# A fused convolution, attention and mixture-of-experts kernel: experts in units of two tiles, with results added to the output by scatter

## What is computed

```python
gate_logits = x_flat @ gate_w.T
topk_vals, topk_idx = jax.lax.top_k(gate_logits, 2)
topk_w = jax.nn.softmax(topk_vals, axis=-1)
...
for e in range(8):
    h = jax.nn.gelu(x_flat @ w1[e].T + b1[e], approximate=False)   # 256 -> 1024
    y = h @ w2[e].T + b2[e]                                        # 1024 -> 256
    out = out + comb[:, e:e + 1] * y
...
t = t + _L1_ffn_ref(_ln_t(t), ...)      # t after the third block is called x3 below
```

## Time and profile before

| | |
|---|---|
| time before, median of 3 runs | 2082.64 us (2081.46 to 2082.74) |
| the profiled execution's own time | 2077.95 us |
| its span, first to last instruction | 2076.1 us |
| busy in the span: PE, DVE, ACT, POOL | 77%, 67%, 40%, 51% |
| front (until the logits are copied) | 0 to 1397.4 us |
| routing (until `TAB` is written) | to 1444.1 us |
| experts (until the last matmul) | to 2029.5 us |
| combination and stores | to 2076.1 us |

### The profile page before, as it was taken

One profiled execution on the slowest core, in us unless ns is written; L12 is line 12 of the kernel. 1 busy time (PEld: TensorE's weight loads), 2 busy tenths in 40 slices (PEclk: granted clock), 3 DMA queues, 4 the chain that ended last, 5 costly groups with the idle time before them and its releaser, 6 DMA issues. The chain is left out here.

```text
span 2076.1 us, 22252 instructions
## 1 busy us (share of the span) xinstructions
PE 1594.2 (77%) x5692; PEld 891.2 (43%) x5693; DVE 1389.0 (67%) x1482; ACT 829.7 (40%) x1496; POOL 1061.4 (51%) x676
## 2 busy tenths in 40 slices
PE   5377778867777867677876777572999999999991
PEld 2122225522224542223452222351676767676760
DVE  2799997689997689998779999637222222222225
ACT  7444436635333754442663533230222222323222
POOL 0799880389893359896149988100223232322210
PEclk9699999979999979999989999785999999999995
DMA  3265540255461146552027555712101011110107
GB/s 112 76 238 199 194 141 21 79 206 207 167 210 43 39 162 204 201 200 86 21 95 246 199 175 173 309 65 82 36 30 35 31 33 33 33 33 32 34 21 265
DMA packets 77416, 247.42 MB, mean 119 GB/s; under 512 B 10812, under 2 KB 24517, under 8 KB 72454
## 3 DMA queue, kind: packets, MB, share of 16 engines
q1 hardware_dynamic: 70502, 227.69, 31.4%
q0 software_dynamic: 6816, 18.62, 2.8%
HBM read 220.72 MB, written 23.99 MB: 118 GB/s over the span
## 5 line engine op out<-in xcount | busy, mean ns | idle before, releaser
L390 PE MATMUL psum<-HC_sb,ident_sb 128*128 128x512 f32 x1024 | 494.2, 607 | 65.1 <-DVE HC_sb L1362 56.8
L390 PE MATMUL psum<-experts_sb 64*128 64x512 f32 (+5 forms) x962 | 313.5, 550 | 232.4 <-DVE HC_sb L1362 144.3
L952 ACT ACTIVATE psum<-experts_sb 128x1024 f32<-128x1024 f32 x256 | 285.4, 1117 | 508.5 <-DVE experts_sb L1352 395.4
L1352 DVE TENSOR_TENSOR_SCAN experts_sb<-psum,DBX_sb 128x1024 f32<-128x1024 f32 x172 | 389.8, 2276 | 32.3 <-POOL DBX_sb L1042 31.3
L390 PEld LDWEIGHTS psum<-HC_sb,ident_sb 128*128 128x128 f32 x1024 | 190.5, 192 | 282.4 <-issue 132.3
L390 PEld LDWEIGHTS psum<-experts_sb 64*128 64x128 f32 (+5 forms) x962 | 98.2, 152 | 469.4 <-DVE HC_sb L1362 239.3
L1738 ACT ACTIVATE hgt_sb<-psum_moe,b_sb 128x128 f32<-128x128 f32 x568 | 154.6, 383 | 359.1 <-PE psum_moe L1688 359.0
L1651 PE MATMUL psum_moe<-experts_sb,hgt_sb 128*128 x1136 | 259.4, 382 | 4.2 <-ACT hgt_sb L1738 2.8
L1651 PE MATMUL psum_moe<-experts_sb,XGT_sb 128*128 x568 | 257.6, 597 | 0.3 <-issue 0.3
L1621 POOL DMA_INDIRECT y_rows<-YS_sb,iy_sb x71 | 70.8, 998 | 356.9 <-PE psum_moe L1672 221.9
L1651 PEld LDWEIGHTS psum_moe<-experts_sb,hgt_sb 128*128 128x128 f32 x1136 | 216.4, 191 | 66.7 <-issue 40.7
(11 more groups left out here) (253 smaller groups left out, 1914.7 us busy)
## 6 DMA issues: line engine op xcount, KB each, us to landing
DA_sb<-bc_rows SPq DMA_DIRECT2D x128, 512.0 KB, 4.6
experts_sb<-bc_rows SPq DMA_DIRECT2D x64, 512.0 KB, 3.7
SQ_sb<-bc_rows SPq DMA_DIRECT2D x64, 512.0 KB, 4.2
X_XT_sb<-bc_rows SPq DMA_DIRECT2D x64, 512.0 KB, 5.4
experts_sb<-w1T SPq DMA_DIRECT2D x8, 1024.0 KB, 19.4
experts_sb<-w2T SPq DMA_DIRECT2D x8, 1024.0 KB, 21.4
experts_sb<-y_rows SPq DMA_DIRECT2D x8, 1024.0 KB, 11.8
X_sb<-x_tok SPq DMA_DIRECT2D x5, 1024.0 KB, 7.0
```

What stands on the lines that cost most here:

```text
L390: return nc.tensor.matmul(o, lhsT, rhs, start=start, stop=stop, **k)
L952: nc.scalar.activation(decays[i % 2], DT[:, c, :], ACT.Exp, scale=a_neg[:, s:s + 1]).then_inc(da_ready, 1)
L1352: v.tensor_tensor_scan(STATE[i % STATE_SLOTS], decays[i % 2], DRIVE[i % STATE_SLOTS], 0.0, ALU.mult, ALU.add).then_inc(h_ready, 1)
```

## The change

- The output is a row for each token (`out`, 4,352 rows of 256 with 256 spare rows for empty slots). `store_x3` writes x3 straight into it, in rows of 1 KB. `x3_dram`, `y_rows` and the whole combination are gone: no loads by SP, no P1 and P2 steps on ScalarE and VectorE, no final stores.
- The gate weights of all slots are laid down in DRAM once: TensorE transposes `P21`, VectorE copies it, SP stores it to `gate_rows` (8,192 values). For each tile a further indirect DMA, `gather_gate`, brings its 128 gate weights, 4 bytes each, to a column of `PS`.
- `result` adds b2 as before and then multiplies by the gate weight (a second VectorE instruction). `scatter_add` adds the 128 rows to `out` in DRAM (`compute_op=ALU.add`). A token has two results, in two tiles, so each scatter waits until the one before has landed (`added`).
- The 71 tiles make 39 units: `PAIRS` = 32 units of two tiles of one expert and 7 units of one tile. `TE` holds the expert of each unit. The routing has more steps for it (42 counted steps become 56).
- `up` is turned round: 128x128 pieces of W1 are the stationary operand and the rows `XGT` (256 columns, 128 in a single unit) the moving one, 16 matmuls for a unit. The hidden values come out with the hidden index on the partitions, as `down` needs them, so `turn_hidden` and the copy to `hg` are gone, and GELU reads PSUM directly (8 pieces of 128x256 for a unit).
- The stationary pieces are read from `W1S`, to which VectorE copies the expert's W1 for every unit (`copy_weights`, 128x2048), two units ahead.
- POOL's instructions are all written out, with the columns of `TAB`, `GIX` and `SCAT` given directly; the copies to `ix` and `iy` are gone. The gathers of the unit four ahead stand between the scatters.

```diff
-                sp.dma_start(x3_dram[b], X2[:, :, :]).then_inc(stored, 16)
+                sp.dma_start(out[0:TOK, :].rearrange("(b n p) c -> b p n c", n=NB, p=P)[b], X2[:, :, :]).then_inc(stored, 16)
...
-            def gather(tile, k):
-
-                nc.gpsimd.tensor_copy(IX[:, k:k + 1], TAB[:, bass.ds(tile, 1)]).then_inc(ix_ready, 1)
-                pool.wait_ge(ix_ready, tile + 1)
-                pool.sem_inc(indices_there, 1)
...
+            def gather(tile):
+                k = slots(tile)
+                if tile >= 4:
+                    pool.wait_ge(t1_ready, (tile // 2 if tile < 2 * PAIRS else tile - PAIRS) - 1)
                 pool.indirect_dma_start(XG[:, k, :], None, xm_rows,
+                                        bass.IndirectOffsetOnAxis(ap=TAB[:, tile:tile + 1], axis=0)).then_inc(xg_ready[k], 16)
+
+            def gather_gate(tile):
+                pool.indirect_dma_start(PS[:, tile:tile + 1], None, gate_rows,
+                                        bass.IndirectOffsetOnAxis(ap=GIX[:, tile:tile + 1], axis=0)).then_inc(
+                                            gate_there[slots(tile)], 16)
+
+            def scatter_add(tile):
+                pool.wait_ge(y_done, tile + 1)
+                if tile:
+                    pool.wait_ge(added, tile * 16)
+                pool.indirect_dma_start(out, bass.IndirectOffsetOnAxis(ap=SCAT[:, tile:tile + 1], axis=0),
+                                        YS[:, tile % 4, :], None, compute_op=ALU.add).then_inc(added, 16)
...
+            for tile in range(4):
+                gather(tile)
+            pool.wait_ge(tab_done, 2)
+            pool.wait_ge(gates_stored, 16)
+            for tile in range(8):
+                gather_gate(tile)
+                if tile >= 4:
+                    gather(tile)
+            for u in range(UNITS):
+                for j in range(2):
+                    if j < width(u):
+                        scatter_add(first_tile(u) + j)
+                    if u + 4 < UNITS and j < width(u + 4):
+                        gather(first_tile(u + 4) + j)
+                        gather_gate(first_tile(u + 4) + j)
...
+            def up(u, k):
+                w = width(u) * P
+                pe.wait_ge(w1_copied, u + 1)
+                pe.wait_ge(xgt_done, u + 1)
                 for h in range(NH):
-                    for c in range(CT):
-                        m = mm(psum[:, h, :], XGT[:, k2, c, :], W1[:, bass.ds(e, 1), c, h * HL:(h + 1) * HL],
-                               c == 0, c == CT - 1)
+                    if not isinstance(u, int) or u:
+                        pe.wait_ge(gelu_done, u * 2 + (h - 1))
+                    for q in range(4):
+                        for c in range(CT):
+                            m = mm(psum[:, 2 * h + q // 2, (q % 2) * 2 * P:(q % 2) * 2 * P + w],
+                                   W1S[:, k, c, (4 * h + q) * P:(4 * h + q + 1) * P], XGT[:, k, c, 0:w],
+                                   c == 0, c == CT - 1)
+                    m.then_inc(m1_ready, 1)
...
+            def step(u, k, ready):
+                turn_rows(u + 1, (k + 1) % 2, ready)
+                up(u, k)
+                down(u - 1, (k + 1) % 2)
...
+            def copy_weights(u, k):
+                e = dve.value_load(TE[0:1, bass.ds(u, 1)], min_val=0, max_val=E - 1)
+                if not isinstance(u, int) or u >= 2:
+                    dve.wait_ge(m1_ready, u * 2 - 2)
+                v.tensor_copy(W1S[:, k, :, :].unsqueeze(1), W1[:, bass.ds(e, 1), :, :]).then_inc(w1_copied, 1)
...
+                dve.wait_ge(gate_there[there[1]], there[2])
+                dve.wait_ge(y_biased, tile + 1)
+                v.tensor_scalar(ys, ys, PS[:, bass.ds(tile, 1)], None, ALU.mult).then_inc(y_done, 1)
```

More of the change, by code:

```diff
@@ L1513, in lay_out, with build_moe @@
     return a
-def build_moe(nc, t, x3_dram, xm_rows, y_rows, logits, routing, experts, out):
+def build_moe(nc, t, xm_rows, gate_rows, logits, routing, experts, out):
     with ExitStack() as ctx:
@@ L1548, in build_moe @@
+        STARTS = sb("starts", [P, 2, E])
+        TEC = sb("tec", [P, UNITS, 2 * E])
+        TEF = sb("tef", [P, UNITS])
+        TEI = sb("tei", [P, UNITS], U32)
+        TE = sb("te", [P, UNITS], mybir.dt.int32)
         ROWF = sb("rowf", [P, NT])
         EMPTY = sb("empty_row", [P, NT])
[L1550 to L1555, removed]
@@ L1585, in build_moe, with width, first_tile, slots @@
         C_ALL = 16 * len(consts)
+        def width(u):
+            return 2 if not isinstance(u, int) or u < PAIRS else 1
+        def first_tile(u):
+            return 2 * u if not isinstance(u, int) or u < PAIRS else u + PAIRS
+        def slots(tile):
+            return tile % 4 if tile < 2 * PAIRS else 2 * ((tile - PAIRS) % 2)
+        def uses(tile):
+            return sum(slots(i) == slots(tile) for i in range(tile + 1))
         @block.sync
@@ new lines, in turn_rows @@
+            def turn_rows(u, k, ready):
+                for j in range(width(u)):
+                    pe.wait_ge(xg_ready[2 * k + j], ready)
+                if not isinstance(u, int) or u >= 2:
+                    pe.wait_ge(xgt_done, u - 1)
+                for j in range(width(u)):
+                    for c in range(CT):
+                        m = nc.tensor.transpose(psum[:, 6 + k, c * 2 * P + j * P:c * 2 * P + (j + 1) * P],
+                                                XG[:, 2 * k + j, c * P:(c + 1) * P], ident[:, :])
@@ L1851, in _ @@
[L1851 to L1863 removed]
+            table_step(v.tensor_copy(ROWF[:, :], TAB[:, :]))
@@ L1882, in _ @@
[L1882 to L1900 removed]
+            rows_turned(2, 0)
@@ new lines, in _ @@
+            copy_weights(2, 0)
+            for j in range(2):
+                result(0, j, (j, j, 16), None)
+            rows_turned(3, 1)
+            copy_weights(3, 1)
+            for j in range(2):
+                result(1, j, (2 + j, 2 + j, 16), None)
+            with dve.Fori(1, PAIRS // 2 - 1) as i:
+                for k in range(2):
+                    rows_turned(i * 2 + (k + 2), k)
+                    copy_weights(i * 2 + (k + 2), k)
+                    for j in range(2):
+                        result(i * 2 + k, j, (2 * k + j, 2 * k + j, i * 16 + 16), i * 64 + (32 * k + 16 * j - 48))
@@ L1903 @@
+            for u in range(PAIRS - 2, UNITS):
+                if u + 2 < UNITS:
+                    rows_turned(u + 2, u % 2)
+                    copy_weights(u + 2, u % 2)
+                for j in range(width(u)):
+                    tile = first_tile(u) + j
+                    result(u, j, (tile % 4, slots(tile), 16 * uses(tile)), 16 * (tile - 3))
 def kernel(**inputs):
```

343 lines of the change are left out of this document (142 added, 201 removed).

## The result

The changed kernel takes **1981.85 us** (median of 4 runs, 1980.77 to 1983.14), the kernel before 2082.05 on the same chip (4 runs, 2081.11 to 2082.74). The ratio is 0.9517, 95% interval 0.9504 to 0.9530: 100 us less. The profiled execution took 1983.14 us with a span of 1981.2.

A forecast was written before the change was run, and what follows sets the result against it. Routing bound by a VectorE chain, the expert stage by TensorE, the end by DMAs and VectorE; -60.7 - 9.4 + 5.1 + 1.1 - 40.6 - 0.9 = -105.4 us, so 2082.64 - 105.4 = 1977.2 us; 8-in-10 range 1966 to 2005.

The forecast's parts named there:

- a sum of -105.4: Whole kernel: gains and losses of all stages added up to 105.4 us less.
- The likeliest case: Whole kernel: 1977.2 us for the median, 5% faster; chance 0.82.
- Three stages with three limits: Whole kernel before: VectorE chain in 53.4 us of routing, TensorE in the expert stage, DMAs and VectorE in the 46.6 us tail.
- TensorE's work: Expert stage: 32 pairs at 14.24 us and 7 single units at 7.17, 505.9 instead of 566.6, gain 60.7 us.
- the rival of the dear turned `up`: Expert stage: narrower moving side costs more per column, some 1.7 us a tile, about 2120 us in all; chance 0.01.
- Cover: Expert stage: VectorE, ScalarE and POOL work and TensorE's waits stay hidden under a pair unit's 14.24 us.
- Routing and start: Before the first `up`: routing 3.5 us longer, first `up` 5.1 us later in all (3.9 to 6.3).
- The wait for the gather of tile 5: Start of the expert stage: TensorE waits about 1.1 us (0 to 4.3) for this gather, POOL's 12th DMA.
- The adding scatter's L: Expert stage and end: an adding scatter's landing time, taken as 4.2 us between 2.4 and 5.2, chain 5.0 a tile, hidden.
- The slower rival: Expert stage: adding scatter is the bound, landing over 7.8 us eats the whole gain; 2240 us at 10; chance 0.05.
- The end: After the last matmul: 6.0 us to the span's end instead of 46.6, gain 40.6 us.

The follow-up runs named there:

- e1: The kernel before with only `up` turned round, tiles single and the old combination at the end, plus two more x3 images loaded there: 2026.12 us.
- e12: The changed kernel with reordered first gathers, two PSUM banks by turns for single tiles, and bias multiplied by gate early: median 2.1 us below the changed kernel's.
- e8: The changed kernel with the first gathers reordered, rows of tiles 0 to 5 before the gates: median 2.8 us below the changed kernel's.
- e6: The changed kernel with one more unused gate gather per tile from tile 8 on, waited for at the end: median 1981.77 us.
- e7: The changed kernel with three more gate gathers per tile from tile 8 on, waited for at the end: median 2067.11 us.
- e11: The changed kernel with the copies of the first weights to `W1S` on ScalarE instead of VectorE: median 1978.89 us.
- e2: The changed kernel with x3 stored into a tensor of its own, as the kernel before stores it, so the output lacks x3: median 1983.58 us.
- e9: The changed kernel with a one-column memset on GpSimd ahead of its first gather: drain 8.44 us from the last scatter's start, total time not given.
- e3: The changed kernel with the scatters writing instead of adding: median 1984.47 us, drain 10.10 us.
- e5: The changed kernel without the 71 gate gathers, all results weighed with 0.5: stage 2.0 us shorter, drain 5.87 us, total time not given.
- e10: The changed kernel with a one-column memset on GpSimd behind the last scatter: drain ends 8.55 us behind that scatter's start, total time not given.
- e4: The changed kernel with GpSimd waiting for the last adding scatter's landing before its drain: median 3.4 us above the changed kernel's.

## Why the prediction was right, and where it was off

The forecast was 1977.2 us for the median from a sum of -105.4, and the measured time is 1981.85, a gain of 100.2 to 100.8 against the two medians of before. The likeliest case came true, and no rival decided the time.

- **What bounds.** Three stages with three limits held, and TensorE kept the middle.
- **TensorE's work.** Pair 14.24 forecast, 14.25 measured; single tile 7.17 forecast, 7.25 in e1. That a record of 256 moving columns costs half of one of 512 settled the rival of the dear turned `up`. By the figures of the Trainium skill (TensorE: Matmul & The Clock Gate, Back-to-back issue gap), about 81 ns at 128 columns and 131 at 512, the prediction's estimate was a time near 2120. The measurement decides: e1, which has this part alone, took 2026.12 us, and its records of 128 columns come every 3.57 / 32 = 0.11 us, about half of the 0.2155 at 256.
- **Cover.** Every cover named held: no wait of TensorE for VectorE, ScalarE or a gather between 1471 and 1966. The one I had excused wrongly is the last `down`: I gave `y_biased` 7.3 us from the unit before, but at the very end two `down` follow each other and there is none. It put the last matmul off by 0.7 us, though not the end, as e12 shows, where the last scatter waits for the landing of the one before.
- **Routing and start.** From the logits' copy to the end of `TAB` it is 50.4 us against 47.0, +3.4 for 3.5 forecast. The first `up` starts, counted from the front's end, 0.3 us sooner than forecast. The wait for the gather of tile 5 was 1.9, not 1.1, and e8 shows that it is that gather's.
- **POOL.** In a row of gathers without a wait most are 1.25 us apart (0.95 and 0.30), the first two 1.47 and 1.81, where I took 1.4; a scatter of 1.6 to 2.5 us was not foreseen, since I priced every transfer at 0.98 us. It stayed hidden, and e6 and e7 show by how much: one transfer more for a tile fits, three do not. The Trainium skill (SBUF — State Buffer, Who interferes with whom) has a rule for the longer ones: an f32 copy from SBUF to SBUF on VectorE and GpSimd's writing of descriptors shut each other out. e11 and e1 agree with it; here it costs a scatter up to 0.9 us.
- **The adding scatter's L.** By the landings in the trace it is 3.9 us in the median of the 71, up to 4.8 in the second scatter of a pair beside the VectorE copy, and 3.7 to 3.8 for the last two, where I took 4.2. The slower rival needed over 7.8. In 27 of the 32 pairs the second scatter starts 0.79 us behind the landing of the first, so inside a pair the chain of landings does set the pace; two such chains fit in 14.25 us, as forecast.
- **The end.** This is the step that was off. "L 4.2: the span ends" left out that the end also waits for GpSimd's drain. In the kernel before the drain ended at 2034.8, and 41 us of other work ran on beside and behind it, so the earlier trace rows could not show it. By moving POOL's last transfer to the end of the program, the change uncovered it. From the last matmul to the end it is 10.0 us and not 6.0, although the parts that I did list came to 5.1: their 0.9 us too much hid part of the miss.

In the profiled execution that adds up. The forecast end of the span was 1970.7; a front that ended 4.6 later, 1.9 more on TensorE to its last matmul (0.8 of the gap, 0.7 of the last `down`, the rest in small pieces), and 4.0 more at the end give 1981.2, which is the measured span. In the medians, where the front's spread should count for less, the 5.9 us of the last two stand against a miss of 4.65.

**What stays open** is what sets the length of the drain. It is the same to 0.01 us in six kernels: 8.44 in the changed one, e2, e9 and e11, which have the same transfers on GpSimd, and 3.92 in the kernel before and e1. That speaks for something in the program, but e8 and e12, whose program for GpSimd is also the same, differ by 0.12 (7.86 and 7.97). Adding does not make it long (e3), the number of transfers alone does not set it (e5), and neither moving the code by one place (e9) nor a memset ahead of it (e10, 0.11 us) does much. The order of the first gathers moves it (e8), plain scatters in place of adding ones make it longer (e3), and so does a wait ahead of it (e4). A kernel whose last tile does not go through a GpSimd transfer was not tried.

## What to carry to other kernels

Read per stage what TensorE's time consists of: a transposition that exists only since one matmul puts its result the wrong way round can be removed by swapping the operands, and that is priced by records of two widths in the same trace. A combination at the end can be scattered in as the tiles come, if the chain of landings (here 4.5 to 4.8 us from one scatter to the next) fits well under the bound's pitch (7.1). And when an engine's last work moves to the end of the program, ask what that engine still does after its last instruction: the trace of before hides it under other work.

## What the runs showed of the hardware that was not expected

- GpSimd's drain ends 3.9 to 10.9 us behind the start of its last transfer, though that lands after 2.4 us where it is plain and after 3.7 to 3.9 where it adds; in the changed kernel 4.6 us of it lie bare.
- An adding scatter of 128 rows of 1 KB takes 1.6 us on POOL in the median where a plain one takes 1.0 (e3). Beside a VectorE copy of 128x2048 it takes up to 2.5 (gone in e11), and a plain one 1.7 in the mean (e1).
- A gap of 2.8 us on TensorE can cost more than itself: the mean clock behind one was 0.81, and the next 32 records took 8.25 us instead of 7.07 (e7). Later in the same trace gaps as long left the clock at 1.00.
- The end of the front differs by up to 8 us between executions, so that in this kernel gains of 2 us are read from stretches of the trace and not from the total.
